# Moving three kinds of work inside a slot of a fused Mamba-2 and LoRA block on Trainium2

## What is computed

```
xn = layernorm(x)                                     # x: 1024 tokens x 512
proj = xn @ in_proj_w.T                               # gate 8192 | hs 8192 | B 1024 | C 1024 | dt 128
hBC = silu(causal_conv4(proj[hs, B, C]) + conv_b)
dt = clip(softplus(dt + dt_bias), 0, 100);  A = -exp(A_log)
# 128 heads of 64 in 8 groups of B and C (128 states), 8 chunks of 128 tokens:
Y = (C B^T * L) (hs * dt) + C state * exp(A_cum) + hs * D        # L: the decay inside a chunk
g = Y * silu(gate)
out = rmsnorm(g, over groups of 1024 channels) * norm_w
result = x + out @ out_proj_w.T + base(xn) + top-2-of-8 LoRA(xn)
```

## Time and profile before

| | |
|---|---|
| median of 3 runs | 1800.57 us |
| the profiled execution | 1797.44 us |
| its span, first to last instruction | 1796.1 us |
| mean granted TensorE clock | 0.991 of full speed |
| busy: PE, DVE, ACT, POOL | 94%, 77%, 69%, 60% of the span |

### The profile page before, as it was taken

One profiled execution on the slowest core, in us unless ns is written; L12 is line 12 of the kernel. 1 busy time (PEld: TensorE's weight loads), 2 busy tenths in 40 slices (PEclk: granted clock), 3 DMA queues, 4 the chain that ended last, 5 costly groups with the idle time before them and its releaser, 6 DMA issues.

```text
span 1796.1 us, 32206 instructions
## 1 busy us (share of the span) xinstructions
PE 1688.6 (94%) x11244; PEld 1355.8 (75%) x11244; DVE 1381.9 (77%) x1793; ACT 1246.5 (69%) x2687; POOL 1082.6 (60%) x1037
## 2 busy tenths in 40 slices
PE   6979999999999999999999999999999999999988
PEld 4767777787777877778777777778777787777766
DVE  6768778886887878887778877887687877878765
ACT  5167676776767777676776777777667777677775
POOL 3036467665676656665567556765566755776575
PEclk9989999999999999999999999999999999999999
DMA  3242143332433234332333324342343323433142
GB/s 122 91 148 93 62 145 127 120 108 88 133 124 120 86 101 143 120 124 75 131 120 135 98 78 151 112 142 87 100 133 116 130 76 103 143 124 104 65 141 95
DMA packets 97167, 202.57 MB, mean 113 GB/s; under 512 B 28392, under 2 KB 29936, under 8 KB 92784
## 3 DMA queue, kind: packets, MB, share of 16 engines
q1 hardware_dynamic: 97008, 200.51, 33.6%
HBM read 162.20 MB, written 38.28 MB: 112 GB/s over the span
## 4 chain that ended last, share of the span: by engine, by line
PE 68%; DVE 16%; POOL 6%; ACT 5%; issue 5%; DMA 0%; DVEq 0%; ACTq 0%; SPq 0%; POOLq 0%
PE P L241 20%; PE P L243 19%; PE P L242 18%; DVE hsX L641 5%; PE P L400 5%; POOL GL L884 4%; DVE hsX L647 2%; PE P L287 2%; PE P L417 2%; DVE Bx L641 1%; ACT P L475 1%; DVE P L846 1%; DVE yb L849 1%; DVE EM L682 1%; POOL yb L932 1%
## 5 line engine op out<-in xcount | busy, mean ns | idle before, releaser
L932 POOL TENSOR_TENSOR yb<-yb,dhs 128x512 f32<-128x512 f32 x112 | 144.2, 1287 | 412.0 <-DVE yb L824 412.0
L475 ACT ACTIVATE P<-AB,SC 128x128 f32<-128x128 f32 x1024 | 308.7, 370 | 0.0
L241 PE MATMUL P<-xh,AH 128*128 128x512 f32 x656 | 270.2, 412 | 37.8 <-DVE hsX L641 32.3
L641 DVE SCALAR_TENSOR_TENSOR hsX<-P,cwt,hsX 128x1023 f32<-128x1023 f32 (+2 forms) x192 | 245.5, 1279 | 18.1 <-ACT hsX L441 13.6
L243 PE MATMUL P<-xh,AL 128*128 128x512 f32 x656 | 257.4, 392 | 0.0
L242 PE MATMUL P<-xl,AH 128*128 128x512 f32 x656 | 257.2, 392 | 0.0
L618 ACT ACTIVATE tg<-P 128x512 f32<-128x512 f32 x127 | 76.0, 598 | 255.2 <-PE P L243 255.2
L241 PE MATMUL P<-GH,xh 128*128 128x512 f32 x544 | 220.7, 406 | 16.2 <-POOL GL L884 16.2
L241 PE MATMUL P<-OH,gTh 128*128 128x512 f32 x512 | 213.8, 418 | 2.3 <-issue 2.2
L243 PE MATMUL P<-GH,xl 128*128 128x512 f32 x544 | 214.0, 393 | 0.0
L242 PE MATMUL P<-GL,xh 128*128 128x512 f32 x544 | 213.7, 393 | 0.0
(11 more groups left out here) (181 smaller groups left out, 4067.7 us busy)
## 6 DMA issues: line engine op xcount, KB each, us to landing
AB<-acr_d SPq DMA_DIRECT2D x128, 512.0 KB, 4.9
AR<-in_wa SPq DMA_DIRECT2D x80, 256.0 KB, 2.8
TS<-in_wg SPq DMA_DIRECT2D x16, 1024.0 KB, 5.0
TS<-in_wo SPq DMA_DIRECT2D x16, 1024.0 KB, 5.4
part_d<-pl SPq DMA_DIRECT2D x64, 256.0 KB, 3.2
pl<-part_d SPq DMA_DIRECT2D x64, 256.0 KB, 2.7
al<-acc_d SPq DMA_DIRECT2D x64, 256.0 KB, 3.0
acc_d<-al SPq DMA_DIRECT2D x58, 256.0 KB, 2.2
```

Source lines behind the costliest of these rows:

```text
L241: te.matmul(o, ah_, bh_, start=(first and i == 0), stop=False)
L475: r = se.activation(E[:, h, :], AB[m % 2][:, h, :], ACT.Relu, bias=SC[s % 2][:, c, 3, h:h + 1], scale=-1.0)
L641: ve.scalar_tensor_tensor(out=o[:, d:T], in0=raw[:, 0:T - d], scalar=cwt[:, n, 3 - d:4 - d], in1=o[:, d:T], op0=ALU.mult, op1=ALU.add).the ...
L932: pe_.tensor_tensor(yb[:, :], yb[:, :], dhs[:, :], ALU.add).then_inc(s_tp, 1)
```

## The change

Five moves, with the order of the PE list unchanged:

- ACT makes the high parts GH of the next gate weights at the end of chunk 6, ahead of AH, the tanh and the next hsr, and no longer in chunk 7 behind the Exp.
- POOL makes the low parts GL in chunk 7 ahead of the addition to yb.
- The low parts OL of the output weights move from DVE (end of chunk 0) to POOL (start of chunk 1, ahead of the addition to yb). They become a plain subtraction. For it ACT multiplies TS by the norm weights in place, with four more instructions, each behind its OH.
- DVE's gate comes behind the Off product (L824).
- DVE's silu product comes ahead of EM, and no longer between the gating (L849) and the convolution.

```diff
@@ act_program, in the loop over m
-                    if c == 7 and s + 1 < NS:
-                        se.wait_ge(s_gt, m + 1)
-                        act_gate_hi(s + 1)
...
                     if c == 0:
                         se.wait_ge(ts_in, 16 * (3 + 2 * s))
                         for j in range(4):
-                            se.activation(OH[:, j, :], TS[:, j, :], ACT.Copy, scale=nwt[:, 4 * s + j:4 * s + j + 1]).then_inc(s_oh, 1)
+                            nw_ = nwt[:, 4 * s + j:4 * s + j + 1]
+                            se.activation(OH[:, j, :], TS[:, j, :], ACT.Copy, scale=nw_).then_inc(s_oh, 1)
+                            se.activation(TS[:, j, :], TS[:, j, :], ACT.Copy, scale=nw_).then_inc(s_oh, 1)
+                    if c == 6 and s + 1 < NS:
+                        act_gate_hi(s + 1)
                     for i in done:
                         act_ring(i + 4)
@@ dve_program, in the loop over m
-                    dve_gate(m)
                     o = bank("St", m) if c != 7 else None
                     if c:
...
                         ve.tensor_tensor(h8(yb[:, :]), h8(bank("Off", m)), bc(SC[s % 2][:, c, 1, :]), ALU.mult).then_inc(s_t1, 1)
+                    dve_gate(m)
...
                         ve.tensor_tensor(S[:, :], o, S[:, :], ALU.add).then_inc(s_st, 1)
+                    for k in slot_halves[m]:
+                        if k % 2:
+                            dve_silu(k // 2)
                 if m + 1 < M:
                     dve_decay(m + 1)
...
                     ve.tensor_tensor(yb[:, :], bank("Y", m), tg[:, :], ALU.mult).then_inc(s_g, 1)
-                    for k in slot_halves[m]:
-                        if k % 2:
-                            dve_silu(k // 2)
...
-                    if c == 0:
-                        for j in range(4):
-                            ve.wait_ge(s_oh, 4 * s + j + 1)
-                            ve.scalar_tensor_tensor(out=OL[:, j, :], in0=TS[:, j, :], scalar=nwt[:, 4 * s + j:4 * s + j + 1],
-                                                    in1=as_f(OH[:, j, :]), op0=ALU.mult, op1=ALU.subtract).then_inc(s_ol, 1)
@@ POOL
+        def pool_out_lo(s):
+            for j in range(4):
+                pe_.wait_ge(s_oh, 8 * s + 2 * j + 2)
+                pe_.tensor_tensor(OL[:, j, :], TS[:, j, :], as_f(OH[:, j, :]), ALU.subtract).then_inc(s_ol, 1)
...
                 if m < M:
+                    if c == 7 and s + 1 < NS:
+                        pool_gate_lo(2 + s)
+                    if c == 1:
+                        pool_out_lo(s)
                     if c:
                         pe_.wait_ge(s_t1, n0(m))
                         pe_.wait_ge(s_dhs, m + 1)
                         pe_.tensor_tensor(yb[:, :], yb[:, :], dhs[:, :], ALU.add).then_inc(s_tp, 1)
-                    if c == 7 and s + 1 < NS:
-                        pool_gate_lo(2 + s)
```

## The result

The changed kernel takes 1849.99 us (median of 4 runs, 1848.28 to 1851.31), the kernel before 1799.74 us on the same chip. The ratio is 1.0278, with a 95% interval of 1.026 to 1.0296. The forecast was 1836 us, with a range up to 1849: the direction held, and the time is 14 us over the forecast, 1 us outside the range.

What follows compares the result with a forecast made beforehand. PE was taken as the bound, busy 1688.6 of 1796.1 us. The terms 10 + 25 + 2 + 0 - 1 = +36 us on 1797.4 gave 1833.4, and 1836 us for the median, with a range of 1808 to 1849 us.

Steps and rivals of the forecast that it cites:

- the wait for GL replaced by one for the gated result: Chunk 7 of even groups: GTr waits for the gated result instead of GL, -0.1 us, 7 times.
- The ordinary slots: Slots where gate and silu product moved: costs and gains cancel, together 0 us, between -8 and +10.
- the turn of chunk 7: Chunk 7 of odd groups into the next group: hsr, Exp and convolution later, PE's A +0.3 us, 7 times.
- 7 x 3.6: Chunk 1 of odd groups: late hsr and POOL's late yb move the convolution from 684.81 to 688.4, +25 us in all.
- St starts 1.3 us later: 8 x 1.3: Chunk 1 of even groups: the products on ACT delay hsr, xch and dxh, and so St, +10 us in all.
- Rival 4: Slots with a convolution don't regain 0.65 us, chunk 7's late Exp costs 1 us a turn: +50 us, 1850 us; chance 0.05.
- it begins at 761.8 in place of 760.14 and ends at 765.7, and PE's A, which started at 765.35 without a wait, starts at 765.7: Slot 5.7: the late Exp delays the convolution, and its end delays PE's A by 0.3 us, 7 times.
- (1): Chunk 1 of odd groups: four OL fit before yb is wanted, POOL isn't late; 10 us less, 1827 us; chance 0.18.
- The odd turn's 3.6 us: Chunk 1 of odd groups: the convolution ends at 688.4 against 684.81, from late hsr and POOL's late addition to yb.
- (2): Faster if the four products take under 2.0 us: chunk 7 regains GL's waits, 23 us, OL's leaving 10; chance 0.09.
- 653.95 with the silu product of Bx between them: Slot 4.7 on POOL: the four GL end at 652.8, or 653.95 if DVE's silu product falls among them.
- OL's leaving DVE to be worth nothing: Chunk 1 of even groups: DVE is freed to no use, since xch waits for the later hsr.

Runs made afterwards that it cites:

- e_al_first: The changed kernel with DVE's output sum al ahead of the convolution in chunk 7 of odd groups: 1849.62 us, ratio 1.0279.
- e_products_dve: The changed kernel with the four in-place products kept on ACT, but OL made by DVE at the end of chunk 0: 1832.15 us, ratio 1.0182.
- e_gh_only: The kernel before with only GH made at the end of chunk 6 and GL ahead of the addition to yb in chunk 7: 1789.3 us, ratio 0.9944.
- e_fill_both: The changed kernel with redundant matmuls filling PE's waits in chunk 1 of both odd and even groups: 1841.79 us, ratio 1.0238.
- e_fill: The changed kernel with 9 redundant matmuls in chunk 1 of each odd group only: 1850.83 us, ratio 1.0278.

## Why the prediction was wrong by 14 us

The mechanisms at the turns were right, and so were their sizes: 1.27 us in chunk 1 of even groups (1.3), 3.5 us in chunks 1 to 3 of odd groups (3.6), 2.1 us in 15.1 (Y starts 8.07 us behind GTr in place of 5.96), the wait for GL replaced by one for the gated result. The ordinary slots were put at nothing and came out at +0.6 us. Two things failed: the granted clock, put at nothing, by 9.5 us (14.5 in the changed kernel less the 5.0 that the kernel before loses and the changed one doesn't), and the turn of chunk 7 by 5.8.

**The granted clock.** The sum's step "7 x 3.6", and "St starts 1.3 us later: 8 x 1.3" likewise, counts a stall of PE as its length and no more. Seven of the stalls that it made longer, and the one in 14.7, were followed by matmuls at the lower clock. Filling the waits of chunk 1 with matmuls takes 10.9 us of it back at unchanged starts of St, 8 us net of the fillers that weren't hidden (1841.8 us); 15.1, whose wait was not filled, kept its loss. No rival had it. The sum also took over the profiled execution of the kernel before as it was, with 5.0 us at the lower clock in it. Rival 4's 1850 us fits the total by luck: its turn of chunk 7, 1 us each, is what was measured (1.1), but its larger term, the slots with a convolution, came out near nothing, and the clock filled its place.

**The turn from 5.7 to 6.0, +7.8 in place of +2 us.** The step was "it begins at 761.8 in place of 760.14 and ends at 765.7, and PE's A, which started at 765.35 without a wait, starts at 765.7". The convolution was nearly as late as said, 1.42 us and not 1.66: counted from the GTr before (764.23 - 12.77 = 751.46 before, 770.04 after), it began at 8.68 before and begins at 10.10. Its end at 14.01 would hold up an A that began at 13.89 by 0.2 us. But behind the convolution DVE has al, and al frees the bank of the B product, which PE does ahead of A. A begins at 15.02, 1.13 us later, 7 times. The step looked at A's wait alone and not at the bank's. Putting al first gives only 0.24 of it back, for it then pushes the convolution by its own 0.66 us. With al first PE's wait for the bank is gone and the one for the convolution is what remains: `e_al_first` shows the bank as what ended last here, and that this exchange is no cure.

Of the rivals, (1) failed, since Y plus yb did wait for POOL (1.35 us). The odd turn's 3.6 us were made up of 2.2 for hsr and 1.4 for POOL; measured are 1.7 with the products alone (`e_products_dve`, against the kernel before) and 1.8 more with POOL's row, so its sum was better than its parts. (2) failed at its condition, the products took 2.45 us. But its first half, that chunk 7 gives PE back what it waited for GL, is true for even groups (1.05 us each in `e_gh_only`), and only the silu product among GL hid it. The prediction had that: "653.95 with the silu product of Bx between them".

The forecast took OL's leaving DVE to be worth nothing, since hsr is later. Against the kernel before that is right. Against the same kernel with OL on DVE the move costs 54 us, 17 more than the forecast's 37. Of these the clock in seven slots is 13 and OL's 0.83 us of lock, which the other moves win in 7 turns, 6; 15.1 and the odd turns give 1 to 2 back.

What stays open: which of the turns gets the lower clock. The same wait of 3.27 us was followed by it in one even group of the changed kernel, in six with the filler in the odd ones, and in four with al first, and the same 2.05 us in 14.7 in the changed kernel and in `e_fill_both`, but not in `e_fill`. The Trainium skill ("TensorE: Matmul & The Clock Gate", section "Part 1: The HAM clock gate") says that the gate has only the two levels and that what it looks at isn't tied to the program's start. The traces agree with the first, matmuls of 512 columns start 0.23 or 0.43 us apart. The second would let the same wait be hit in one turn and spared in the next; no run here shows that it is the reason.

## What to carry to other kernels

Moving work to an engine with room costs what stands behind it in that engine's list and in front of the next reader: four short ACT instructions ahead of the copy that everything waits for cost 37 us, the subtractions themselves 10 alone and 17 behind them. When parts of a change have mixed signs, run them apart: two parts of this one come out 10 us faster each, and a version without the harmful ones is 1.2% faster than the kernel before. And look at the granted clock slot by slot, in the kernel before too: behind a longer turn it is part of the price, and of the 10 us that each of these two parts seems to win, 5 are turns of the kernel before that ran at the lower clock.

## What the runs showed of the hardware

- After PE's waits of 2 to 3.4 us at a turn, the granted clock was at its lower level for some us in part of the turns, which cost 1.5 to 2.65 us each; the 5.05 us in 15.1 cost 2.0. In the kernel before, waits for GL of 1.24 us and less at three turns were followed by it and cost 1.65 us each. With 9 redundant matmuls in the wait in odd groups it was gone there and came in even groups; with both waits filled it was gone from both.
- DVE's instructions with two SBUF operands and POOL's on SBUF stretched each other at three places: OL 3.57 us beside al and 2.74 alone; GL 6.02 us beside a silu product and 5.04 alone; the silu product 2.32 us there.
